# Attention scores from split queries and keys, in an image encoder layer on one core

## What is computed

```python
q = silu(x @ Wq)   # 16 heads of 64
k = silu(x @ Wk)
v = x @ Wv
decay = exp(where(causal, cum_i - cum_j, -inf))
attn = einsum('bhid,bhjd->bhij', q, k) * decay
o = einsum('bhij,bhjd->bhid', attn, v)
# then a group norm over (sequence, head width), a sigmoid gate, @ Wo, residual,
# layer norm, router, top 2 of 8 experts with a hidden width of 1024
```

## Time and profile before

| | |
|---|---|
| Median of 3 runs | 1227.42 us (1226.4 to 1227.95) |
| The profiled execution | 1226.3 us |
| Its span, from the first to the last instruction | 1224.3 us |
| TensorE busy | 1203.5 us, 98% |
| ScalarE busy | 870.4 us, 71% |
| VectorE busy | 842.0 us, 69% |
| GpSimd busy | 427.7 us, 35% |
| Mean granted TensorE clock | 0.997 |

### The profile page before, as it was taken

How to read it: one execution, slowest core, us unless ns; L and a number is a source line. 1 busy time by engine, 2 the same in 40 slices (tenths; PEclk the granted TensorE clock), 3 DMA queues, 4 the chain that set the end, 5 groups by cost and what they waited for, 6 DMA issues and landing times. The chain is left out here.

```text
span 1224.3 us, 27609 instructions
## 1 busy us (share of the span) xinstructions
PE 1203.5 (98%) x8634; PEld 1064.1 (87%) x8634; DVE 842.0 (69%) x2156; ACT 870.4 (71%) x2046; POOL 427.7 (35%) x521
## 2 busy tenths in 40 slices
PE   8899999999999999999999999999999999999997
PEld 6788788888888888888888788889999999999996
DVE  5655666776776776776766577568888888466663
ACT  5777767767767767767668658447888888666663
POOL 2211221242242242242242141464544445443433
PEclk9999999999999999999999999999999999999999
DMA  6533223242242342342333238398987886999984
GB/s 199 185 101 96 84 97 102 77 139 89 89 141 81 97 141 80 97 127 94 97 108 104 91 122 276 114 281 230 267 252 212 243 228 191 257 273 258 286 250 99
DMA packets 125609, 194.48 MB, mean 159 GB/s; under 512 B 16272, under 2 KB 91504, under 8 KB 125360
## 3 DMA queue, kind: packets, MB, share of 16 engines
q1 hardware_dynamic: 110864, 175.37, 45.1%
q0 software_dynamic: 13584, 17.26, 7.0%
q10 hardware_dynamic: 1056, 0.55, 0.2%
HBM read 167.40 MB, written 29.05 MB: 160 GB/s over the span
## 5 line engine op out<-in xcount | busy, mean ns | idle before, releaser
L1274 PE MATMUL bank<-xn_sp,big_r 128*128 128x512 f32 x1152 | 297.6, 401 | 1.4 <-DVE dec_x L1823 0.9
L1274 PEld LDWEIGHTS bank<-xn_sp,big_r 128*128 128x128 f32 x1152 | 208.9, 189 | 48.6 <-issue 2.1
L698 POOL TENSOR_SCALAR_AFFINE_SELECT dec_x<-dec_x 128x256 f32<-128x256 f32 x256 | 112.0, 465 | 358.7 <-DMA dec_x<-cum_scratch 358.5
L892 ACT ACTIVATE dec_x<-dec_x,ncum 128x256 f32<-128x256 f32 (+1 forms) x512 | 186.5, 446 | 11.9 <-issue 7.9
L1622 PE MATMUL bank<-big_r 128*128 128x256 f32 x1296 | 167.9, 286 | 0.8 <-ACT q_s L963 0.8
L1622 PEld LDWEIGHTS bank<-big_r 128*128 128x128 f32 x1296 | 160.6, 192 | 2.0 <-ACT q_s L963 1.0
L1823 DVE TENSOR_TENSOR dec_x<-bank,dec_x 128x384 f32<-128x384 f32 x256 | 126.3, 550 | 50.7 <-PE bank L1319 31.7
L755 POOL DMA_INDIRECT out<-mid_f,tok x68 | 114.2, 1680 | 61.2 <-DMA out<-mid_f,tok 24.2
L749 POOL TENSOR_SCALAR mid_f<-mid_f,dec_x 128x256 f32<-128x256 f32 x68 | 73.0, 1078 | 160.6 <-DVE mid_f L2086 157.1
L963 ACT ACTIVATE mid_f<-bank,h 128x256 f32<-128x256 f32 x216 | 101.3, 478 | 31.9 <-PE bank L1622 19.0
L2118 DVE TENSOR_TENSOR big_r<-mid_f,big_r 128x256 fp32r<-128x256 f32 x216 | 91.4, 424 | 42.6 <-ACT big_r L983 41.0
(11 more groups left out here) (260 smaller groups left out, 2348.2 us busy)
## 6 DMA issues: line engine op xcount, KB each, us to landing
big_f<-in_L_ffn_w SPq DMA_DIRECT2D x68, 1024.0 KB
dec_x<-cum_scratch SPq DMA_DIRECT2D x128, 384.0 KB
big_w<-in_L_ffn_w SPq DMA_DIRECT2D x12, 1024.0 KB, 8.4
mid_f<-expert_rows SPq DMA_DIRECT2D x27, 261.0 KB
h_scratch<-h SPq DMA_DIRECT2D x16, 256.0 KB
h<-h_scratch SPq DMA_DIRECT2D x8, 512.0 KB, 4.1
out<-h SPq DMA_DIRECT2D x16, 256.0 KB, 4.4
xt<-in_x SPq DMA_DIRECT2D x14, 256.0 KB, 3.7
```

What stands on the lines that cost most here:

```text
L698: pool.affine_select(out=d, in_=d, pattern=[[0, 2], [1, P]], compare_op=ALU.is_ge, fill=fill, base=0, channel_multiplier=-1).then_inc(M["c ...
L892: act.activation(d, d, ACT.Exp, bias=ncum[p % 2][:, NS * u + s, 2 * c + hh:2 * c + hh + 1]).then_inc(M["exp_done"], 1)
L1274: mm = pe.matmul(bank[target][:, :], wp[:, k, c * P:(c + 1) * P], xp[:, k, :], start=(k == 0 and j == 0), stop=(k == EC - 1 and j == 2))
```

## The change

The scores are formed as three fp32r products of split queries and keys. `q_s` and `k_s`, two buffers each, give way to `q_f`, `q_hi`, `q_lo`, `k_f`, `k_hi` and `k_lo`, one buffer each. ScalarE gets `query_hi` (one copy of 128 x 512) and `key_hi` (two of 128 x 256, one for each image); VectorE gets `query_lo` (one subtraction of 128 x 512) and `key_lo` (two of 128 x 256). The scores wait for the low parts (`sl_done`) and the silus for all scores of the step before. In steps 2 and 3 the values go behind the keys. Some exponentials of steps 4 and 5 go ahead of `key_hi`, some other work of VectorE changes its place about `key_lo`, and three semaphores are merged into others.

```diff
             def scores(p, c, u):
                 n = 4 * (NP * p + c) + 2 * u
-                pe.wait_ge(M["sq_done"], NP * p + c + 1)
-                pe.wait_ge(M["sk_done"], NP * p + c + 1)
+                pe.wait_ge(M["sl_done"], 3 * (NP * p + c) + 2 + u)
...
-                q, k = (x[c % 2][:, u * S:(u + 1) * S] for x in (q_s, k_s))
-                for hh in range(2):
-                    r = slice(D * hh, D * hh + D)
-                    pe.matmul(score_bank(p, c, u, hh)[:, 0:S], k[r, 0:P], q[r, :], start=True, stop=True)
-                for hh in range(2):
-                    r = slice(D * hh, D * hh + D)
-                    pe.matmul(score_bank(p, c, u, hh)[:, S:LW], k[r, P:S], q[r, P:S], start=True, stop=True).then_inc(M["s_ps"], 1)
+                qk = three([x[:, u * S:(u + 1) * S] for x in (k_hi, k_lo)], [x[:, u * S:(u + 1) * S] for x in (q_hi, q_lo)])
+                for j, (k, q) in enumerate(qk):
+                    for hh in range(2):
+                        r = slice(D * hh, D * hh + D)
+                        pe.matmul(score_bank(p, c, u, hh)[:, 0:S], k[r, 0:P], q[r, :], start=(j == 0), stop=(j == 2))
+                for j, (k, q) in enumerate(qk):
+                    for hh in range(2):
+                        r = slice(D * hh, D * hh + D)
+                        mm = pe.matmul(score_bank(p, c, u, hh)[:, S:LW], k[r, P:S], q[r, P:S], start=(j == 0), stop=(j == 2))
+                        if j == 2:
+                            mm.then_inc(M["s_ps"], 1)
...
+            def query_hi(p, c):
+                n = NP * p + c
+                act.wait_ge(M["sq_done"], n + 1)
+                have(act, "s_ps", 4 * n)
+                act.activation(q_hi[:, :], q_f[:, :], ACT.Copy).then_inc(M["sh_done"], 1)
+
+            def key_hi(p, c):
+                n = NP * p + c
+                act.wait_ge(M["sk_done"], n + 1)
+                have(act, "s_ps", 4 * n)
+                for u in range(2):
+                    act.activation(k_hi[:, u * S:(u + 1) * S], k_f[:, u * S:(u + 1) * S], ACT.Copy).then_inc(M["sh_done"], 1)
...
+            def query_lo(p, c):
+                n = NP * p + c
+                dve.wait_ge(M["sh_done"], 3 * n + 1)
+                dve.tensor_tensor(q_lo[:, :], q_f[:, :], f32(q_hi[:, :]), ALU.subtract).then_inc(M["sl_done"], 1)
+
+            def key_lo(p, c):
+                n = NP * p + c
+                for u in range(2):
+                    cols = slice(u * S, (u + 1) * S)
+                    dve.wait_ge(M["sh_done"], 3 * n + 2 + u)
+                    dve.tensor_tensor(k_lo[:, cols], k_f[:, cols], f32(k_hi[:, cols]), ALU.subtract).then_inc(M["sl_done"], 1)
```

The lists of the engines, in the order of a step. ScalarE:

```diff
                 tanh_q(p, c + 1)
                 if c == 0 and p > 0:
                     keep_v(p, 2, 2)
-                if c in (1, 2, 3):
-                    keep_v(p, {1: 4, 2: 6, 3: 7}[c], 2)
+                if c == 1:
+                    keep_v(p, 4, 2)
                 if c == 3 and post:
                     y_hi(p - 1, 1, 1)
+                query_hi(p, c + 1)
                 tanh_k(p, c + 1)
                 if c == 0 and p > 0:
                     keep_v(p, 3, 2)
-                if c == 1:
-                    keep_v(p, 5, 2)
+                if c in (1, 2, 3):
+                    keep_v(p, c + 4, 2)
+                if c == 4:
+                    decay(p, c + 1, 1, (0,))
+                if c == 5:
+                    decay(p, c + 1, 0, (0,))
                 if c == 6 and nxt:
                     keep_cum(p + 1)
+                key_hi(p, c + 1)
+                if c == 6 and nxt:
                     xn_hi(p + 1)
...
                 if late:
-                    decay(p, c + 1, 0)
-                decay(p, c + 1, 1)
+                    decay(p, c + 1, 0, (1,) if c == 5 else (0, 1))
+                decay(p, c + 1, 1, (1,) if c == 4 else (0, 1))
```

VectorE and TensorE:

```diff
+                query_lo(p, c + 1)
                 silu_k(p, c + 1)
+                if c == 0 and post:
+                    affine(2 * p - 1)
+                if c == 4 and nxt:
+                    decay_logits(p + 1)
+                if c == 5:
+                    affine(2 * p)
+                    if nxt:
+                        log_decay(p + 1)
+                key_lo(p, c + 1)
                 if c == 0:
-                    if post:
-                        affine(2 * p - 1)
                     if nxt:
                         embed(2 * p + 2)
...
-                if c == 2:
-                    values(p, 6, 2, "tg_done", NP * p + 4)
-                if c == 3:
-                    values(p, 7, 2, "tg_done", NP * p + 5)
...
                 keys(p, c + 1)
...
+                if c in (2, 3):
+                    values(p, c + 4, 2, "tg_done", NP * p + c + 2)
```

More of the change, by code:

```diff
@@ L159, in vit_layer @@
         yo = [mid_f[:, 2 * BS * EW + NGEL * BLK + i * BS * E:2 * BS * EW + NGEL * BLK + (i + 1) * BS * E].rearrange("p (s n) -> p s n", s=BS) for i in range(2)]
-        q_s = [sb(f"q_s{i}", [P, SP2]) for i in range(2)]
-        k_s = [sb(f"k_s{i}", [P, SP2]) for i in range(2)]
+        with nc.sbuf_tensor("q_hi", [P, SP2], F32R) as q_hi:
+            pass
+        q_1 = sb("q_1", [P, SP2])
+        with nc.sbuf_tensor("q_lo", [P, SP2], F32R) as q_lo:
+            pass
+        q_f = sb("q_f", [P, SP2])
+        with nc.sbuf_tensor("k_hi", [P, SP2], F32R) as k_hi:
+            pass
+        k_1 = sb("k_1", [P, SP2])
+        with nc.sbuf_tensor("k_lo", [P, SP2], F32R) as k_lo:
+            pass
+        k_f = sb("k_f", [P, SP2])
         tq = sb("tq", [P, SP2])
@@ L238, in vit_layer @@
         w1_stage = [w1_f[0], w1_x]
-        gel_u = [x[:, i * BLK:(i + 1) * BLK] for x in q_s + k_s for i in range(2)]
+        gel_u = [x[:, i * BLK:(i + 1) * BLK] for x in (q_1, q_f, k_1, k_f) for i in range(2)]
         gel_1 = [gel_u[c // 2][:, (c % 2) * P:(c % 2 + 1) * P] for c in range(HC)]
@@ L883, in keep_v, with decay @@
                 act.activation(v_sb[:, t, n * 512:(n + 1) * 512], bank[source][:, :], ACT.Copy).then_inc(M["v_done"], 1)
-            def decay(p, c, u):
+            def decay(p, c, u, heads=range(2)):
                 n = 2 * NP * p + 2 * c + u
                 act.wait_ge(M["causal"], 2 * (n + 1))
-                act.wait_ge(M["ncum_done"], p + 1)
-                for hh in range(2):
+                act.wait_ge(M["ncum_done"], 2 * (p + 1))
+                for hh in heads:
                     for s, cols in ((0, slice(0, S)), (1, slice(S, LW))):
@@ L996, in last_step @@
                     keep_v(p + 1, 0, 2)
+                    query_hi(p + 1, 0)
                     tanh_k(p + 1, 0)
                     keep_v(p + 1, 1, 2)
+                    key_hi(p + 1, 0)
                     decay(p + 1, 0, 0)
@@ L1084, in _ @@
                 keep_v(0, i, 2 + i)
+            query_hi(0, 0)
             tanh_k(0, 0)
+            key_hi(0, 0)
             tanh_g(0, 0)
@@ L2133, in last_step @@
                     y_lo(p, 0, 1)
+                    query_lo(p + 1, 0)
                     silu_k(p + 1, 0)
+                    key_lo(p + 1, 0)
                     first_half(p, 0)
@@ L2211, in step @@
                     y_lo(p - 1, 1, 1)
[L2212 to L2220 removed]
+                if c == 4 and not nxt:
+                    first_places()
                 if c == 6:
@@ L2242, in _ @@
             weight_lo(3)
+            query_lo(0, 0)
             silu_k(0, 0)
+            key_lo(0, 0)
             dve.wait_ge(M["g_in"], 16 * 7)
```

37 lines of the change are left out of this document (13 added, 24 removed).

## The result

The changed kernel takes 1285.96 us (median of 4 runs, 1281.57 to 1288.16), the kernel before 1226.91 us (4 runs on the same chip, 1224.99 to 1227.95): a ratio of 1.0473, with an interval of 1.0454 to 1.0492. It is slower by 59 us. The forecast was 1272 us within 1240 to 1300. The profiled execution took 1287.8 us with a span of 1285.8, 61.5 us more than before.

The account below looks back on a forecast made before the run. TensorE, busy 98%, bounds the kernel, its helpers' answers coming just in time. Six full pairs 31 us, first and last pair 12, scores 6: 49, taken as 45, so 1272 us, range 1240 to 1300.

Parts of the forecast that it names:

- the scores' own cost: Score products on TensorE: 0.705 us an image as three fp32r products against 0.66 in fp32, 6 us more over all.
- Step 6: Late ScalarE, query_hi ahead of tanh_k, query_lo ahead of silu_k, then the key splits: following scores start 1.8 us later.
- Step 2: silu_q ends late, then the splits stand on the path: the scores that follow start 1.6 us later.
- Step 5: As step 6 without affined: query_hi and query_lo hold the keys, and the following scores start 1.2 us later.
- Step 1: embed and the multiplications start later behind step 0's key_lo, so the queries come 0.4 us later.
- The tail: key_hi, then key_lo of the first image, between silu_k and the scores: 1.07 us where it was 0.10.
- the first and the last pair: Less work between and more steps where silu_k is just in time: 6 us lost in each.
- rival (a): Short products not held by their weight loads: scores -15 instead of +6 us, waits stay, 1251 us; chance 0.14.
- Rival (c): fp32r matmuls of the two heads don't run side by side: +90 us, about 1345 us; chance 0.09.
- Rival (d): The waits and a load-free scores stage cancel, within 0.2% of the kernel before; chance 0.05.
- Rival (b): Passes decide: scores take three quarters, 21 us less, and idle ScalarE and VectorE absorb the splits, 1206 us; chance 0.10.
- Step 2's slack: The 1.4 us that moving the values behind the keys should give in step 2 lies unused, as silu_q ends late.

Follow-up runs that it names:

- filler: Changed kernel with fp32r products on constants into an unused bank ahead of the scores' wait, filling TensorE's waits: 1280.39 us, ratio 1.0419.
- pe_only: Kernel before, with silus written in fp32r and scores as three fp32r products of the same unsplit operands, no splits: 1230.27 us, ratio 1.0017.
- mixed_two: Changed kernel's order with fp32 scores, but three products for the 256-column part in steps 0 and 5, with only the splits these need: 1226.01 us, ratio 0.9979.
- load_only: Changed kernel with fp32 scores waiting for the silus alone; the six split instructions read a constant table and wait for no other engine: 1240.43 us, ratio 1.0107.
- splits_none: Changed kernel's order, single buffers and merged semaphores, but no splits and plain fp32 scores: 1226.94 us, ratio 0.9996.
- fp32_scores: Changed kernel with all splits made in place but unread; scores in fp32 waiting for the silus alone: 1268.77 us, ratio 1.034.
- values_back: Changed kernel with values 6 and 7 put back ahead of the keys in steps 2 and 3: 1292.65 us, ratio 1.0515.

## Why the prediction was right, and where its sizes were off

**Direction and place: right. The weights of the parts: not.** The time lies 14 us above the forecast and inside the range. TensorE's idle time stands ahead of the scores that follow steps 2, 5 and 6 (1.22, 0.88 and 1.51 us in pair 3) and is put down to `k_lo`, and a full pair takes 98.2 us where 98 to 99 stood.

**The terms of a full pair.** Predicted 5.1 us, measured 5.14, but that exactness is luck: the measured number also holds the scores' own cost, for which the prediction had 0.75 us a pair on top. Step 6: 1.8 predicted, 1.61 measured, and its four parts 0.5, 0.5, 0.1 and 0.7 were 0.43, 0.47, 0.11 and 0.59. Step 2: 1.6 and 1.24. Step 5: 1.2 and 0.97. Step 1: 0.4 and 0.84. Steps 0, 3, 4 and 7: 0.1 and 0.48, nearly all in step 3. The tail, from the end of `silu_k` to the scores, is 0.97 us, predicted 1.07. What was too large and what was too small cancelled. In step 1 the second half of the queries starts 347.11 - 342.72 = 4.39 us after the step's start, before 319.04 - 315.00 = 4.04, so what the prediction had worked out there is 0.35; the other 0.49 come behind it and had no term. The row of TensorE:

```profile
347.11 1.63 PE L1307 MATMUL bank<-xn_sp,big_r 128*128 128x512 f32 x6 [0.20 <-DVE dec_x L1869]
```


**The term that was mis-sized: the first and the last pair.** "I give them 6 us each": 12.0 and 8.8 were measured. The sum had four steps at 1 to 1.8 us. In pair 0 seven of the eight steps lose 1.2 us or more, step 5 alone 2.95 (10.62 for 7.67), of which filler gives back 1.5. In pair 7 it is four steps, 2, 3, 5 and 6, but at 2.0, 2.8, 2.0 and 1.9 us; a stretch at 1.2 GHz begins in its step 3. Beside them, the work ahead of the first scores (+3.5) and the part behind the last (+4.2) weren't priced at all. Together that is 28.5 us for 12. The prediction had no term for the clock. By filler it is about 6.5 us: 2.0 in pair 0, 4.2 behind the last scores, which is all that was lost there, and 1.7 in pair 2, where the clock had fallen once, less 1.3 that the other parts lose with the fillers.

**The scores' own cost.** "the scores cost [...] 6 us more over all": the start of the scores to that of what follows grew by 0.015 us a step in the trace, 1 us over 64; pe_only has 2. The 0.115 us for the 128-column products were right for all but the first of each three, which came after 0.06 to 0.07. That the width hardly counts was right, and rival (a) falls with it: the second and third pair of 128 columns take what one of 256 takes. That it is the load which holds them fits the rows, but no run shows it. Rival (c) falls with the heads side by side, the two records of a pair mostly within 4 ns of each other and never over 34. Rival (d), waits and cheaper scores that cancel, falls with 4.7%.

**Rival (b), passes decide.** It had the scores at three quarters. They took 1.53 us for 1.51, with three products for two fp32 ones of two records each. So nothing of the 21 us came in, and even if the helpers had absorbed the splits, nothing would have been won at this mix of widths. The rule of the Trainium skill ("FP8 and Floating Point Precision", TensorE Precision Notes) that true FP32 takes four passes would give three quarters of the time if an fp32r product takes one; this trace doesn't agree, with 0.46 for 0.54 and 0.40 for 0.43 us at 256 columns and 0.29 for 0.22 at 128. At 256 columns something is won all the same: mixed_two has 0.15 us less in each of its two steps. The part of it that concerns the helpers needs a correction, though. It said that they have 28 and 26 us idle in a pair (VectorE 28, ScalarE 26; the prediction names them the other way round) and can take the work. load_only shows that they can: at the same busy time pair 3 takes 0.80 us more, not 5.1. They can't take it where it stands, with waits for each other.

**The cause in numbers.** Each rung of this ladder adds one thing, the last one two; whole kernel by ratio, and pair 3 against before's 93.07:

| | ratio | pair 3 |
|---|---|---|
| order, single buffers, semaphores (splits_none) | 0.9996 | 93.01 |
| + the load of the splits (load_only) | 1.0107 | 93.87 |
| + the waits between ScalarE and VectorE (fp32_scores) | 1.0340 | 96.89 |
| + the scores' wait and the products (changed) | 1.0473 | 98.21 |

So of 4.7% about 1.1 are the load, 2.3 the blocking and 1.3 the tail with the products, of which pe_only gives the products 0.2. The lowered clock is in these shares, in the last above all: 3.4, 10.2, 13.6 and 37.5 us at half from rung to rung. Pair 3 had the full clock in all four traces, and there it is 0.86 us for the load, 3.02 for the blocking and 1.32 for the tail with the products. The prediction had the pieces but told them as one chain in which the tail was the biggest; the blocking is. The shares hold for this order of adding: steps 5 and 6 together gain 0.9 us when the tail goes, not twice the 0.87 that the tail adds (0.97 - 0.10). The tail without the blocking was not run; I expect that it would have looked larger, added first.

**Step 2's slack** "lies unused": confirmed by values_back. For step 3 the prediction had no term for the moved values, and they are worth 1.05 us there.

**Still open.** Why the part ahead of the first scores grows by 1.5 us in splits_none already (35.65 us for 34.19), from one profile each, was not tried; by its ratio the whole kernel doesn't show it. That part also differs by 0.8 us between the changed kernel and filler (38.51), which have the same work in it, so the +3.5 us ahead of the first scores are rough. Nor was a version tried with `embed` ahead of `key_lo` in step 0, which should give back up to the 0.85 us of step 1 (my estimate, from 12.41 and load_only's 11.56).

## What to carry to other kernels

An idle third of a helper engine is room for work only if that work waits for nothing: the same six instructions cost 0.8 us a pair on ready data and 3.8 as a ping-pong between two engines whose lists run in order. Before adding a split, look at where its operand is ready and what is queued behind its wait; put first on the list what the next producer needs (the tanh and the silu of the keys ahead of the queries' copy and subtraction gave back 20 of 59 us). Where passes are traded for narrower ones, count time from start to start at the real width: here three fp32r products cost more at 128 columns than the fp32 one that they replace, and less at 256, and only there was something to win.

## What the runs showed of the hardware

In the changed kernel fp32r products with 64 rows start every 0.11 to 0.12 us at 256 columns, and so do the second and third ones at 128; the pair behind the first one of 128 columns came after 0.06 to 0.07. So three at 128 columns took 0.29 us where three at 256 took 0.40 to 0.46. Their weight loads took 190 to 196 ns each, in fp32 186. By the Trainium skill ("TensorE: Matmul & The Clock Gate", Weight-path perf modes) the fast weight load is on for 128 weights of a type that isn't FP32; if it was on for fp32r here, the durations of the loads show nothing of it. The heads on partitions 0 to 63 and 64 to 127 ran side by side in fp32r as in fp32.

The granted clock fell to 1.2 GHz in the changed kernel ahead of the first scores, in pairs 0, 2 and 7, and for 10.2 us from the last scores on, a stretch in which TensorE was busy throughout. Ahead of five of the seven stretches TensorE had just stood at `k_lo`, for 2.1, 2.4, 1.3, 1.7 and 2.1 us. In pair 3 it stood there for up to 1.5 us, and the clock stayed at 1.00, so the length of one wait alone doesn't decide it. With filler products in the waits these five stretches were gone; the two others, ahead of the first scores and in the first steps of pair 0, stayed (17 us).

A copy of 128 x 512 on ScalarE took 629 ns and a subtraction on VectorE 718, the halves 408 and 421.
